# A decoder layer on one core: transposes of the linear-memory stage by VectorE blocks and a DRAM round trip in place of TensorE

## What is computed

```python
x = x + attn(layernorm(x))      # linear memory: sig = elu(q) + 1
#   q   = layernorm(x) @ Wq.T + bq            (8 heads of 128 are used)
#   out = (sig @ M[h]) / (sig . z[h] + eps)   per head, then @ Wo.T
x = x + xattn(layernorm(x), ctx) # 32 query heads, 4 key heads, softmax, @ Wo
x = x + ffn(layernorm(x))        # router, top 8 of 64, expert biases
```

## Time and profile before

| | |
|---|---|
| median of 3 runs (lowest to highest) | 679.18 us (678.88 to 680.33) |
| the profiled execution: its time, its span | 679.2 us, 677.4 us |
| busy: PE, PE weight loads, DVE, ACT, POOL | 668.1, 562.0, 511.7, 401.5, 120.3 us |
| granted TensorE clock, mean | 1.0 of full |
| DMA | 113.26 MB, mean 167 GB/s |

### The profile page before, as it was taken

How to read it: one execution, slowest core, us unless ns; L and a number is a source line. 1 busy time by engine, 2 the same in 40 slices (tenths; PEclk the granted TensorE clock), 3 DMA queues, 4 the chain that set the end, 5 groups by cost and what they waited for, 6 DMA issues and landing times.

```text
span 677.4 us, 11137 instructions
## 1 busy us (share of the span) xinstructions
PE 668.1 (99%) x3394; PEld 562.0 (83%) x3394; DVE 511.7 (76%) x1101; ACT 401.5 (59%) x1224; POOL 120.3 (18%) x132
## 2 busy tenths in 40 slices
...
GB/s 329 348 363 279 31 202 1 0 1 32 78 144 139 208 156 218 172 251 264 240 199 205 179 194 249 261 196 206 192 198 233 184 268 95 87 79 63 63 17 62
DMA packets 100676, 113.26 MB, mean 167 GB/s; under 512 B 6096, under 2 KB 72912, under 8 KB 100624
## 3 DMA queue, kind: packets, MB, share of 16 engines
...
## 4 chain that ended last, share of the span: by engine, by line
PE 85%; DVE 6%; ACT 4%; issue 2%; DMA 1%; SPq 0%; DVEq 0%; ACTq 0%
PE bank L1055 22%; PE bank L1125 21%; PE bank L873 15%; PE bank L1248 7%; PE bank L1027 6%; PE bank L1265 5%; PE bank L864 2%; ACT probs L1690 2%; ACT probs L1706 1%; DVE oT L1874 1%; PE bank L1274 1%; PE bank L1194 1%; PE bank L992 1%; PE bank L914 1%; PE bank L958 1%
## 5 line engine op out<-in xcount | busy, mean ns | idle before, releaser
L1125 PE MATMUL bank<-regA,oT 128*128 128x512 f32 x576 | 135.8, 391 | 2.1 <-DVE oT L1874 2.0
L1690 ACT ACTIVATE probs<-bank,negmax 128x128 f32<-128x128 f32 x256 | 90.2, 378 | 66.6 <-DVE negmax L2332 62.3
L1125 PEld LDWEIGHTS bank<-regA,oT 128*128 128x128 f32 x576 | 107.4, 188 | 26.6 <-DVE oT L1874 4.0
L1055 PE MATMUL bank<-xnT,forms 128*128 128x512 f32 x432 | 107.1, 392 | 0.0
L1055 PEld LDWEIGHTS bank<-xnT,forms 128*128 128x128 f32 x432 | 80.2, 188 | 16.2 <-DVE qbuf L2090 0.2
L1055 PE MATMUL bank<-regC,forms 128*128 128x512 f32 x324 | 82.5, 393 | 0.0
L1055 PEld LDWEIGHTS bank<-regC,forms 128*128 128x128 f32 x324 | 59.9, 188 | 12.0 <-DVE regC L1874 0.2
L873 PE MATMUL bank<-regC,xnT 128*128 128x512 f32 x256 | 68.0, 396 | 0.0
L1248 PEld LDWEIGHTS bank<-k_ring,qbuf 128*128 128x128 f32 x512 | 62.0, 191 | 2.5
L1376 ACT CAST oT<-bank 128x512 fp32r<-128x512 f32 (+1 forms) x66 | 37.7, 577 | 43.4 <-PE bank L1265 37.6
L1248 PE MATMUL bank<-k_ring,qbuf 128*128 128x128 f32 x512 | 62.2, 275 | 0.0
...
## 6 DMA issues: line engine op xcount, KB each, us to landing
q_dram<-qbuf SPq DMA_DIRECT2D x32, 512.0 KB, 3.6
qbuf<-q_dram SPq DMA_DIRECT2D x31, 512.0 KB, 5.7
...
pT_raw<-turns_dram SPq DMA_DIRECT2D x22, 512.0 KB, 5.2
wq_raw<-in_L_xattn_Wq SPq DMA_DIRECT2D x14, 512.0 KB, 4.4
...
raw<-in_L_xattn_Wo SPq DMA_DIRECT2D x12, 512.0 KB, 6.1
...
```

What stands on the lines that cost most here:

```text
L1055: last = nc.tensor.matmul(k_bank[:, :], forms[:, p[1], a, i, c, :], right(b)[:, c, :], start=j == 0, stop=j == 5)
L1125: last = nc.tensor.matmul(bank[7][:, :], oT[:, a, h, :], wo_of(g, b, h), start=h == 0 and i == 0, stop=h == GH - 1 and i == 2)
L1690: last = nc.scalar.activation(dst, keys, ACT.Exp, bias=negmax[:, bb, p:p + 1], accum_out=rowsum[:, bb, p:p + 1])
```

## The change

Fourteen of the sixteen sig quads and six of the eight latent tiles are no longer transposed by TensorE. VectorE transposes them by 32x32 blocks, SyncE writes the blocks to DRAM (four DMAs of 64 KB) and loads them back turned (one of 256 KB), ScalarE takes the high part from SBUF, and **GpSimd** takes the low part, which VectorE took. The last two quads (14, 15) and tiles (6, 7) go by TensorE as before. `sig`, `qb`, the denominators and the scalings of the first fourteen quads are laid out by blocks. The output of a quad comes five steps after its query, not four, query 15 has a step of its own, the high part comes at step `s + 3` for the turned quads and `s + 2` for the last two, and the scaling of a tile's rows (`scale_latent`) stands in the step after its moments. The block buffers lie in `rawk` and in the second half of `raw16`, so `wv` is loaded into the first half of `raw16`, and the 2 MB of output weights are loaded after the last latent is done, ahead of `k_raw`. In the attention steps `sum_u3` moves from the end of the odd step to behind `output_low` of the even one.

```diff
+    sig_dram = nc.dram_tensor("sig_dram", (2, P // SUB, SUB, P // SUB, 4 * SUB), F, kind="Internal").ap()
+    lat_dram = nc.dram_tensor("lat_dram", (2, P // SUB, SUB, P // SUB, 4 * SUB), F, kind="Internal").ap()
...
+        wv_again = raw16[:, 0:2048].rearrange("p (k n) -> p k n", k=KC)
+        LAT_TURNED = NT - 2
-        tr_order += [("latent", t) for t in range(NT)]
+        tr_order += [("latent", t) for t in range(LAT_TURNED, NT)]
...
+        SIG_TURNED = 2 * NT - 2
...
+        def latent_in(i):
+            if i == 2 * NT + 4:
+                return LAT_TURNED - 1
+            t = (i - 11) // 2
+            return t if (i - 11) % 2 == 0 and 0 <= t < LAT_TURNED - 1 else None
...
+        def sig_due(i):
+            return [s for s in range(2 * NT) if s + (3 if s < SIG_TURNED else 2) == i]
...
-            return (i - 4) // 2 if i >= 4 and (i - 4) % 2 else None
+            return (i - 5) // 2 if i >= 5 and (i - 5) % 2 else None
...
+            def store_latent(t):
+                sp.wait_ge(lat_turned, t + 1)
+                for a in range(P // SUB):
+                    sp.dma_start(lat_dram[t % 2, :, :, a, :].rearrange("c j n -> j c n"),
+                                 lat_turns(t)[a * SUB:(a + 1) * SUB, :].rearrange("j (c n) -> j c n", n=4 * SUB))\
+                      .then_inc(lat_stored, 16)
+            def load_latent(t):
+                sp.wait_ge(lat_stored, 64 * t + 64)
+                if t >= 2:
+                    sp.wait_ge(lat_lo, t - 1)
+                sp.dma_start(lat_raw(t), lat_dram[t % 2, :, :, :, :].rearrange("c j a n -> (c j) (a n)"))\
+                  .then_inc(lat_loaded, 16)
+            def turn_sig(i):
+                sp.wait_ge(sig_turned, i + 1)
+                for a in range(P // SUB):
+                    sp.dma_start(sig_dram[i % 2, :, :, a, :].rearrange("c j n -> j c n"),
+                                 sig_turns(i)[a * SUB:(a + 1) * SUB, :].rearrange("j (c n) -> j c n", n=4 * SUB))\
+                      .then_inc(sig_stored, 16)
+                if i >= 7:
+                    (store_latent if i % 2 else load_latent)((i - 7) // 2)
+                sp.wait_ge(sig_stored, 64 * i + 64)
+                if i >= 2:
+                    sp.wait_ge(sig_lo, i - 1)
+                sp.dma_start(sig_raw(i), sig_dram[i % 2, :, :, :, :].rearrange("c j a n -> (c j) (a n)"))\
+                  .then_inc(sig_loaded, 16)
+            turn_sig(0)
+            turn_sig(1)
             sp.wait_ge(tr_done, tr("wo", MH - 1) + 1)
-            load_wkv(0, 1)
-            sp.dma_start(wo_raw, wo_rows[:, 0:GH, :]).then_inc(wo_loaded, 16)
+            for i in range(2):
+                sp.dma_start(wv_again[:, 2 * i:2 * i + 2, :], wv_rows[:, 2 * i:2 * i + 2, :])\
+                  .then_inc(wkv_loaded[0][i], 16)
...
-            sp.wait_ge(sig_tr_done, 2 * NT)
+            for i in range(2, SIG_TURNED):
+                turn_sig(i)
+            load_latent(3)
+            for t in range(4, LAT_TURNED):
+                store_latent(t)
+                load_latent(t)
+            sp.wait_ge(lat_lo, LAT_TURNED)
+            sp.wait_ge(wkv_lo, 3 * KC)
+            sp.dma_start(wo_raw, wo_rows[:, 0:GH, :]).then_inc(wo_loaded, 16)
+            sp.wait_ge(sig_tr_done, 2 * NT - SIG_TURNED)
...
-            for k in range(2, 2 + NT):
-                root(k)
+            for i in range(2 * NT + 5):
+                for s in sig_due(i):
+                    if s < SIG_TURNED:
+                        pool.wait_ge(sig_hi, s + 1)
+                        nc.gpsimd.tensor_tensor(sigT_place(1, s), sigT_source(s), sigT_place(0, s).bitcast(F),
+                                                ALU.subtract).then_inc(sig_lo, 1)
+                if output_in(i) is not None:
+                    root(2 + output_in(i))
+                if latent_in(i) is not None:
+                    t = latent_in(i)
+                    pool.wait_ge(lat_hi, t + 1)
+                    nc.gpsimd.tensor_tensor(latT_place(1, t), latT_source(t), latT_place(0, t).bitcast(F),
+                                            ALU.subtract).then_inc(lat_lo, 1)
...
-                if i < 2 * NT - 1:
+                if i < 2 * NT:
                     memory_query(i)
-                if i == 2 * NT - 2:
-                    memory_query(i + 1)
                 if 1 <= i <= MH - EARLY:
                     memory_weights(i + EARLY - 1)
                 if i < MH - EARLY:
                     memory_transposes(i + EARLY)
-                if i >= 4:
-                    memory_output(i - 4)
-                if 2 <= i < 2 * NT + 2:
+                if i >= 5:
+                    memory_output(i - 5)
+                if SIG_TURNED <= i - 2 < 2 * NT:
                     sig_transposes(i - 2)
                 if i < MH - EARLY:
                     wo_transposes(i + EARLY)
-                if output_in(i) and i < 2 * NT:
-                    latent_transposes(output_in(i) - 1)
-                if i == 2 * NT + 2:
-                    latent_transposes(output_in(i - 1) - 1)
...
+            pe.wait_ge(lat_lo, 4)
...
-                if i >= 2:
-                    tile, quad = divmod(i - 2, 2)
-                    act.wait_ge(sig_tr_done, i - 1)
+                for s in sig_due(i):
+                    tile = s // 2
+                    if s < SIG_TURNED:
+                        act.wait_ge(sig_loaded, 16 * s + 16)
+                    else:
+                        act.wait_ge(sig_tr_done, s - SIG_TURNED + 1)
                     if tile >= 4:
                         act.wait_ge(y_done, tile - 3)
-                    high(sigT[:, 0, 4 * quad:4 * quad + 4, (tile % 4) * P:(tile % 4 + 1) * P],
-                         sig_bank(i - 2)[:, :].rearrange("p (m n) -> p m n", m=4)).then_inc(sig_hi, 1)
+                    high(sigT_place(0, s), sigT_source(s)).then_inc(sig_hi, 1)
                 if 1 <= i <= 2 * NT:
                     s = i - 1
                     act.wait_ge(rden_ready, s + 1)
                     for j in range(4):
...
+                if i and output_in(i - 1) is not None:
+                    scale_latent(output_in(i - 1))
...
-                if i >= 2:
-                    tile, quad = divmod(i - 2, 2)
-                    place = (slice(4 * quad, 4 * quad + 4), slice((tile % 4) * P, (tile % 4 + 1) * P))
-                    dve.wait_ge(sig_hi, i - 1)
-                    low(sigT[:, 1, place[0], place[1]], sig_bank(i - 2)[:, :].rearrange("p (m n) -> p m n", m=4),
-                        sigT[:, 0, place[0], place[1]]).then_inc(sig_lo, 1)
+                for s in sig_due(i):
+                    if s >= SIG_TURNED:
+                        dve.wait_ge(sig_hi, s + 1)
+                        dve.wait_ge(sig_lo, s)
+                        low(sigT_place(1, s), sigT_source(s), sigT_place(0, s)).then_inc(sig_lo, 1)
+                if 1 <= i <= SIG_TURNED:
+                    s = i - 1
+                    dve.wait_ge(sig_scaled, s + 1)
+                    if s == 0:
+                        dve.wait_ge(tr_done, tr("wqa", MH - 1) + 1)
+                    if s >= 2:
+                        dve.wait_ge(sig_stored, 64 * s - 64)
+                    nc.vector.transpose(sig_turns(s), sig[:, s % 3, :]).then_inc(sig_turned, 1)
 
             def add_memory(t):
 
                 nc.vector.tensor_tensor(resid[:, t, :], resid[:, t, :], y_bank(t)[:, :], ALU.add)\
                     .then_inc(y_used, 1)
                 dve.wait_ge(y_used, t + 1)
+                moments(resid[:, t, :])
+            def scale_latent(t):
                 if t >= 2:
-                    dve.wait_ge(tr_done, tr("latent", t - 2) + 1)
-                normalise(2 + t, resid[:, t, :], xn[:, t % 2, :], xn_ready)
+                    dve.wait_ge(lat_turned, t - 1)
+                src, dst = resid[:, t, :], xn[:, t % 2, :]
+                if t < LAT_TURNED:
+                    src = src.rearrange("p (k c j) -> p k c j", k=KC, j=SUB)
+                    dst = dst.rearrange("p (c k j) -> p k c j", k=KC, j=SUB)
+                scaled(2 + t, src, dst, xn_ready)
+            def turn_latent(t):
+                dve.wait_ge(xn_ready, NT + t + 1)
+                if t == 0:
+                    dve.wait_ge(tr_done, tr("wo", MH - 1) + 1)
+                if t >= 2:
+                    dve.wait_ge(lat_stored, 64 * t - 64)
+                nc.vector.transpose(lat_turns(t), xn[:, t % 2, :]).then_inc(lat_turned, 1)
 
+            for i in range(2 * NT + 5):
+                memory_step(i)
+                if i and output_in(i - 1) is not None and output_in(i - 1) < LAT_TURNED:
+                    turn_latent(output_in(i - 1))
+                if output_in(i) is not None:
+                    add_memory(output_in(i))
...
+            scale_latent(NT - 1)
...
@@ step_turned of the vector engine @@
                 for bb in range(2):
                     output_low(n - 2, bb)
+                if t % 2 == 0:
+                    sum_u3(p)
...
```

(1 more changed line is left out.)

114 lines of the change are left out of this document (69 added, 45 removed).

## The result

The changed kernel takes 682.4 us (median of 5 runs, 681.92 to 684.1) where the kernel before takes 679.18: a ratio of 1.0051, 95% interval 1.004 to 1.0061. The forecast was 674.5, with a range of 669.5 to 681.0. Its sign is wrong.

The account below looks back on a forecast made before the run. TensorE was taken as the bound, busy 668.1 of 677.4 us. Removed transposes -9.1, waits +4.1 and +0.2, fold waits +0.9, key weights +1.0 and attention steps -1.8 gave -4.7 us: 674.5, range 669.5 to 681.0.

Parts of the forecast that it names:

- What is removed: Memory stage: fourteen sig groups (6.5 us) and six latent groups (2.6 us) of transposes leave TensorE, -9.1 us.
- The ring: Memory stage: VectorE and ScalarE's chain from bias to block transpose needs 11.25 us per two steps where TensorE needs 10.88.
- the wait at quad 14: TensorE's transposes of quad 14 wait 3.4 us for ScalarE's scalings or GpSimd's low part; with output 11, 4.1 us.
- Output 11: Late in the memory stage, GpSimd's low part delays the start of output 11: 0.7 of the 4.1 us.
- the high part of quad 2 waits for its load: Quad 2's stores stand behind 1.5 MB of weights: about 1.5 us later; 4 us would cost 2.5 more.
- The key weights: Behind 2 MB in the queue, k_raw lands 8 us later, delaying the values of tile 5: +1.0 us.
- Rival D: The 3.4 us wait at quad 14 lowers the clock to 1.2 GHz: 677.2 to 679.9 us; chance 0.10.
- Rival B: The DRAM round trip takes 8.5 us, sig loads miss ScalarE's cast, pairs of steps grow: 682.6 us; chance 0.14.
- Rival C: GpSimd's low part takes 2.6 us; output 11, quad 15 and values of tile 5 wait: 678.6 us; chance 0.13.
- The attention steps: Moving sum_u3 behind the low parts of oT takes 0.6 us off each of three waits: -1.8 us.
- No correction: The profiled execution took 679.2 us and the median is 679.18, so nothing was added to the sum.
- Rival A: VectorE keeps up and the waits at quad 14 vanish but for 0.5 us: 669.7 us; chance 0.13.

Follow-up runs that it names:

- e11: Changed kernel with the low parts of the fourteen turned quads on VectorE, ahead of its block transpose, instead of on GpSimd: 681.93 us.
- e7: Changed kernel with VectorE's block transpose of a quad one step later, behind the next-but-one query's bias, high and low parts also one step later: 680.59 us.
- e8: e7 plus key weights ahead of the last turned latent's stores, and value and key weights in three pieces behind loads of quads 2, 4, 6: 672.87 us.
- e3: Changed kernel with 1.5 MB of value and key weights in three pieces behind loads of quads 2, 4, 6, not ahead of quad 2's stores: 679.74 us.
- e12: Changed kernel with key weights issued before the 2 MB of output weights, both still in their late place: 676.04 us.
- e2: Changed kernel with key weights issued before the stores of the last turned latent, and the 2 MB of output weights last: 677.17 us.
- e14: e10 with VectorE's low part at the start of its step, ahead of the bias: 676.75 us.
- e10: e8 plus ScalarE's high part ahead of relu, last quad's load ahead of the latent's stores, and turned quads' low parts on VectorE instead of GpSimd: 671.28 us.
- e1: Kernel before the change with only the move of sum_u3 in the attention steps: 677.87 us.
- e13: Changed kernel without the move of sum_u3 in the attention steps: 685.06 us.

## Why the prediction was wrong

- **What is removed, -9.1: right.** Steps are 5.44 us apart, and with the waits as read the stage adds up to 0.25 us.
- **The ring: right in size.** 11.18 for two steps where 11.25 was forecast, and the wait at quad 14 was 3.85 where 3.4 was meant. Output 11 waited 2.0 and not 0.7. e11 shows that it is ScalarE's chain, not VectorE's work, that closes the ring; opening it (e7, e8) moved its waits to outputs 11 and 12 and took, by the medians, 1.4 to 1.8 us off, so it is a smaller share than the forecast of those runs gave it.
- **"the high part of quad 2 waits for its load", "about 1.5 later": mis-sized.** ScalarE waited 4.5 us there, and the step took 8.92 for 6.4, 2.5 more. Query 7's bias came 3.0 us later against TensorE than forecast (106.08 for 103.7, in a run that began 0.6 earlier); the other 0.6 is the step with the `sig` of 1.78 us (81.18 to 86.78, 5.60 for 5.0). e3 gives the place as 2.7 us. The prediction had named 4 us as a bound and put 2.5 on it.
- **The key weights, "I take 8 ... +1.0": the step that failed most.** They landed 11.5 us after an issue that was itself 4.5 late, and the values of tile 5 waited 3.5. I had 11.8 us for the 2 MB in hand, and took a mean for what stands behind them; e12 shows that the transfer waits for nearly all of the 2 MB (10.5 us to landing in this run). e2 and e12 give 5.2 and 6.4 us for this place with its slow clock.
- **Rival D came true twice, at 1.7 us each,** beside the forecast and not in its place. It was given 0.10 as a case apart, although the forecast itself contained the wait of 3.4 us on which it hangs. By the Trainium skill ("TensorE: Matmul & The Clock Gate", Part 1) an idle array goes to the lower level; the granted clock of 0.66 and 0.69 behind waits of 3.85 and 3.5 us agrees, and behind the 2.0 us at output 11 it stays at 1.00. What one wait must be for it no run here settles (see e14 in the last section).
- **Rival B gave the time (682.6) but not the mechanism.** Only the casts of quads 2 and 13 waited for a load; a load lands in 2.8 us (forecast 2.7), a store in 1.8 (2.0).
- **Rival C was not seen in its size, but its mechanism was.** GpSimd's low parts take 1.28 to 1.76 us, not 2.6. The delay falls on VectorE: 1.78 us for 0.69 (`sig` of quad 3), 1.35 for 0.28 (a denominator of quad 15). The port rule of the Trainium skill ("SBUF — State Buffer", section "SBUF: two separate sides") has a VectorE operation with two SBUF inputs, or in a 2-port mode, and a GpSimd operation hold each other off for a whole instruction; these rows, with two SBUF inputs, agree. In e8 an operation with one input of 128x4 is held as well (1.20 for 0.17); whether it ran in such a mode no row shows. The prediction had the low part run "mostly beside the transposes" and cost "a few tenths"; beside that `sig` it cost 1.1 us of VectorE. What the collisions cost the changed kernel is not shown: e11, without GpSimd's low parts of the quads, is the same time, and with the ring open e10 is 0.8 us faster by the medians, inside the intervals.
- **The attention steps, -1.8:** e1 shows 1.0 to 1.2, since 1.1 us of the waits stay; beside the changed memory stage it is 1.5 to 1.7 (e13, and the changed kernel itself).
- **"No correction" for the rest:** a gain of 0.9 us at the very end, where the last store lands sooner, was in nobody's sum.
- **Rival A's own sum has a slip:** if the waits go but for 0.5 us, the 0.5 is added back, 674.5 - 4.3 + 0.5 = 670.7 and not 669.7.

Sum of the misses in the stage: early outputs +1.1, output 11 +1.3, quad 14 +0.45, values +2.5, clock +3.4, quad 15 -0.2: 8.55, with a measured stage of +5.9 where the forecast had -2.9 (-9.1, 4.1, 0.2, 0.9, 1.0), a difference of 8.8.
